# Attention scores of four heads as two full-height products instead of three half-height ones

## The reference, cut to what matters

```
def xattn(x, data):                     # 16 heads of 16 columns
    q = (x @ Wq + bq)                   # [16, 256, 16, 16]
    k, v = split(data @ Wkv + bkv)      # [16, 77, 16, 16] each
    scores = einsum('bqhd,bkhd->bhqk', q, k) / sqrt(16)
    return einsum('bhqk,bkhd->bqhd', softmax(scores), v) @ Wp + bp
x = x + xattn(layernorm(x), ctx)
x = x + moe(layernorm(x))               # 8 experts, top 2, hidden width 1024, gated
```

## Time and profile before

| | |
|---|---|
| runs | 932.6 us median of 3 (931.0 to 934.75) |
| the profiled execution | 938.24 us, of which the span is 936.4 us |
| mean granted TensorE clock | 0.989 |
| busy share of PE, DVE, ACT, POOL | 95%, 80%, 69%, 44% |

### The profile page before, as it was taken

One profiled execution on the slowest core, in us unless ns is written; L12 is line 12 of the kernel. 1 busy time (PEld: TensorE's weight loads), 2 busy tenths in 40 slices (PEclk: granted clock), 3 DMA queues, 4 the chain that ended last, 5 costly groups with the idle time before them and its releaser, 6 DMA issues.

```text
span 936.4 us, 19131 instructions
## 1 busy us (share of the span) xinstructions
PE 887.6 (95%) x6174; PEld 795.6 (85%) x6174; DVE 745.0 (80%) x1757; ACT 646.3 (69%) x1297; POOL 408.9 (44%) x649
## 2 busy tenths in 40 slices
PE   4999999999998998999999999999999999999995
PEld 3888878887877876788999989899898998998994
DVE  2688888888878888787979788887877877778783
ACT  3676766767666774775977777867776776777773
POOL 3456576777776575330432240605114234052052
PEclk8899999999999999999999999999999999999998
DMA  6332333342255337643756455827817838466442
GB/s 144 66 67 49 74 85 69 86 99 61 63 128 177 114 118 268 182 112 121 217 121 185 135 155 168 240 94 186 278 45 215 282 68 259 177 178 177 147 79 27
DMA packets 132368, 129.17 MB, mean 138 GB/s; under 512 B 59936, under 2 KB 117152, under 8 KB 132128
## 3 DMA queue, kind: packets, MB, share of 16 engines
q1 hardware_dynamic: 119392, 110.36, 38.7%
q0 software_dynamic: 12864, 17.44, 10.3%
HBM read 102.01 MB, written 25.36 MB: 136 GB/s over the span
## 4 chain that ended last, share of the span: by engine, by line
PE 78%; DVE 11%; issue 3%; ACT 3%; another core or an unknown queue 1%; POOL 1%; SPq 1%; DMA 0%; POOLq 0%; DVEq 0%; ACTq 0%
PE bank L1985 35%; PE bank L2029 18%; PE bank L1820 5%; PE bank L1737 4%; PE bank L1977 3%; PE bank L1755 3%; PE bank L1774 2%; DVE maxes L1238 2%; PE bank L1784 2%; PE bank L2017 1%; PE bank L1954 1%; DVE probs L1244 1%; DVE q_l L1279 1%; PE bank L1792 1%
## 5 line engine op out<-in xcount | busy, mean ns | idle before, releaser
L852 POOL DMA_INDIRECT out_rows<-yo,token x68 | 114.4, 1682 | 384.9 <-ACT yo L1095 319.8
L1985 PE MATMUL bank<-xh,wh 128*128 128x512 f32 (+1 forms) x672 | 234.7, 349 | 5.4 <-DVE gate_in L1610 4.8
L1985 PE MATMUL bank<-xl,wh 128*128 128x512 f32 (+1 forms) x672 | 228.9, 341 | 0.0
L1985 PE MATMUL bank<-xh,wl 128*128 128x512 f32 (+1 forms) x672 | 228.5, 340 | 0.0
L1586 DVE TENSOR_TENSOR wl<-raw,wh 128x1024 fp32r<-128x1024 f32 x126 | 152.4, 1220 | 13.0 <-ACT wh L1026 12.1
L1985 PEld LDWEIGHTS bank<-xh,wh 128*128 128x128 f32 x672 | 127.9, 190 | 20.1 <-DVE gate_in L1610 7.5
L2029 PE MATMUL bank<-wh,hh 128*128 128x256 f32 x496 | 141.9, 286 | 1.7 <-issue 1.3
L1985 PEld LDWEIGHTS bank<-xh,wl 128*128 128x128 f32 x672 | 127.8, 190 | 14.9
L2029 PE MATMUL bank<-wh,hl 128*128 128x256 f32 x496 | 140.4, 283 | 0.0
L2029 PE MATMUL bank<-wl,hh 128*128 128x256 f32 x496 | 140.4, 283 | 0.0
L1985 PEld LDWEIGHTS bank<-xl,wh 128*128 128x128 f32 x672 | 128.2, 191 | 10.8
(11 more groups left out here) (195 smaller groups left out, 1861.6 us busy)
## 6 DMA issues: line engine op xcount, KB each, us to landing
raw<-in_W SPq DMA_DIRECT2D x42, 1024.0 KB
raw<-in_Wo SPq DMA_DIRECT2D x25, 1024.0 KB
whole<-in_W SPq DMA_DIRECT2D x8, 1024.0 KB, 7.6
xs<-in_x SPq DMA_DIRECT2D x32, 128.0 KB, 2.7
out_rows<-x SPq DMA_DIRECT2D x32, 128.0 KB, 1.8
shared<-z_rows SPq DMA_DIRECT2D x7, 520.0 KB
bo_row<-in_bo SPq DMA_DIRECT2D x25, 128.0 KB
k_blocks<-k_parts SPq DMA_DIRECT2D x128, 19.2 KB
```

Source lines behind the costliest of these rows:

```text
L852: e.indirect_dma_start(out=out, out_offset=bass.IndirectOffsetOnAxis(ap=token[j % 4][:, s:s + 1], axis=0), in_=yo[j % 2][:, s, :], in_offs ...
L1985: mm = e.matmul(ps[:, h * cols:(h + 1) * cols], ws[split_before(j) % 2][:, w, c, m * P:(m + 1) * P], xx[j % 2][:, c, 0:cols], start=(h == ...
```

## The change: what it does

- The queries of a batch are kept as `q_parts[P, m, g, SEQ]`: for group `g`, the high part stands on the group's own 64 partitions and the low part on the other 64. ACT writes the high parts in two instructions of 64 partitions instead of one of 128, DVE the low parts likewise, onto the other half of the partitions.
- The keys get two tiles a batch: `k_hi` has the high blocks on both halves of the partitions, `k_lo` the low blocks on the group's own half, zeros on the other. One matmul of 128 rows with `k_hi` gives high by high plus low by high; one with `k_lo` gives high by low. `k_lo` lies in the third part of the expert weight tiles `wh[0]` and `wl[0]`, which is unused in this stage.
- `scores(i, m)` issues four matmuls of 128 rows, two for group 0, then two for group 1. Each group waits for its own bank.
- `spread_keys(b)` issues 24 DMAs instead of 8, each of 16 partitions with 2 runs of 77 numbers. POOL clears four tiles of 1232 columns instead of two.

```diff
+KEY_PIECES = 3 * HPC
...
+        k_hi = [sb(f"k_hi{i}", [P, DC, 2, HPB, CTX], F32R) for i in range(2)]
+        k_lo = [part[0][:, 2, :, :].rearrange("p c n -> p (c n)")[
+            :, 0:DC * 2 * HPB * CTX].rearrange("p (m g h k) -> p m g h k", m=DC, g=2, h=HPB)
+                for part in (wh, wl)]
+        q_parts = [sb(f"q_parts{i}", [P, DC, 2, SEQ], F32R) for i in range(2)]
...
                 for h in range(HPC):
+                    g, j = divmod(h, HPB)
                     part = slice(h * HD, (h + 1) * HD)
-                    e.dma_start(k_blocks[b % 2][part, :, :, h % HPB, :].bitcast(F32),
-                                k_parts[part, :, :, b % 2, :].bitcast(F32)).then_inc(
-                                    f_kblocks[b % 2], 16)
+                    other = slice((1 - g) * HALF + j * HD, (1 - g) * HALF + (j + 1) * HD)
+                    for rows_of, dst, w in ((part, k_hi, 0), (other, k_hi, 0), (part, k_lo, 1)):
+                        e.dma_start(dst[b % 2][rows_of, :, g, j, :].bitcast(F32),
+                                    k_parts[part, w, :, b % 2, :].bitcast(F32)).then_inc(
+                                        f_kblocks[b % 2], 16)
...
-                e.activation(q_h[b % 2][:, :, :], q_t[:, :, :], ACTF.Copy).then_inc(q_high, 1)
+                for g in range(2):
+                    part = slice(g * HALF, (g + 1) * HALF)
+                    e.activation(q_parts[b % 2][part, :, g, :], q_t[part, :, :],
+                                 ACTF.Copy).then_inc(q_high, 1)
...
-                e.wait_ge(q_high, b + 1)
-                e.tensor_tensor(q_l[b % 2][:, :, :], q_t[:, :, :],
-                                q_h[b % 2][:, :, :].bitcast(F32), ALU.subtract).then_inc(q_low, 1)
+                for g in range(2):
+                    part = slice(g * HALF, (g + 1) * HALF)
+                    other = slice((1 - g) * HALF, (2 - g) * HALF)
+                    e.wait_ge(q_high, 2 * b + g + 1)
+                    e.tensor_tensor(q_parts[b % 2][other, :, g, :], q_t[part, :, :],
+                                    q_parts[b % 2][part, :, g, :].bitcast(F32),
+                                    ALU.subtract).then_inc(q_low, 1)
...
-                if u0 >= 2:
-                    e.wait_ge(less_max, u0 - 1)
-                for k, (qs, w) in enumerate(((q_h, 0), (q_l, 0), (q_h, 1))):
-                    for g in range(2):
-                        mm = e.matmul(
-                            score_bank[(u0 + g) % 3][:, 0:HPB * CTX],
-                            qs[b % 2][g * HALF:(g + 1) * HALF, m, s * P:(s + 1) * P],
-                            k_blocks[b % 2][g * HALF:(g + 1) * HALF, w, m, :, :].rearrange(
-                                "p h k -> p (h k)"), start=(k == 0), stop=(k == 2))
-                        if k == 2:
-                            mm.then_inc(scores_mm, 1)
+                for g in range(2):
+                    if u0 + g >= 3:
+                        e.wait_ge(less_max, u0 + g - 2)
+                    for k, ks in enumerate((k_hi, k_lo)):
+                        mm = e.matmul(score_bank[(u0 + g) % 3][:, 0:HPB * CTX],
+                                      q_parts[b % 2][:, m, g, s * P:(s + 1) * P],
+                                      ks[b % 2][:, m, g, :, :].rearrange("p h k -> p (h k)"),
+                                      start=(k == 0), stop=(k == 1))
+                    mm.then_inc(scores_mm, 1)
```

More of the change, by code:

```diff
@@ L373, in build @@
         v_rep = [sb(f"v_rep{i}", [P, KB, VW]) for i in range(2)]
-        k_blocks = [sb(f"k_blocks{i}", [P, 2, DC, HPB, CTX], F32R) for i in range(2)]
-        q_h = [sb(f"q_h{i}", [P, DC, SEQ], F32R) for i in range(2)]
-        q_l = [sb(f"q_l{i}", [P, DC, SEQ], F32R) for i in range(2)]
+        k_hi = [sb(f"k_hi{i}", [P, DC, 2, HPB, CTX], F32R) for i in range(2)]
[3 more added lines that the diff above has]
+        q_parts = [sb(f"q_parts{i}", [P, DC, 2, SEQ], F32R) for i in range(2)]
         v_blocks = [sb(f"v_blocks{i}", [P, KB, BLOCK_HEADS, VW]) for i in range(2)]
@@ L510, in spread_keys @@
                 e.wait_ge(k_low, b // 2 + 1)
-                if b == 0:
-                    e.wait_ge(blocks_ready, 2)
+                if b < 2:
+                    e.wait_ge(blocks_ready, 2 * b + 2)
                 if b >= 2:
@@ L806, in pool_program @@
             for i in range(2):
-                e.memset(k_blocks[i][:, :, :, :, :].bitcast(F32), 0.0).then_inc(blocks_ready, 1)
+                for blocks in (k_hi, k_lo):
+                    e.memset(blocks[i][:, :, :, :, :].bitcast(F32), 0.0).then_inc(blocks_ready, 1)
             e.memset(half[:, :], -0.5).then_inc(half_ready, 1)
@@ L899, in keys @@
                     for fl in f_kblocks:
-                        e.wait_ge(fl, 16 * HPC * t)
+                        e.wait_ge(fl, 16 * KEY_PIECES * t)
                 else:
@@ L922, in queries @@
                 if b:
-                    e.wait_ge(q_low, b)
+                    e.wait_ge(q_low, 2 * b)
                 else:
@@ L1729, in scores @@
                 if s == 0 and m == 0:
-                    e.wait_ge(q_low, b + 1)
-                    e.wait_ge(f_kblocks[b % 2], 16 * HPC * (b // 2 + 1))
+                    e.wait_ge(q_low, 2 * b + 2)
+                    e.wait_ge(f_kblocks[b % 2], 16 * KEY_PIECES * (b // 2 + 1))
                 u0 = 4 * i + 2 * m
-                if u0 >= 2:
-                    e.wait_ge(less_max, u0 - 1)
-                for k, (qs, w) in enumerate(((q_h, 0), (q_l, 0), (q_h, 1))):
-                    for g in range(2):
-                        mm = e.matmul(
-                            score_bank[(u0 + g) % 3][:, 0:HPB * CTX],
-                            qs[b % 2][g * HALF:(g + 1) * HALF, m, s * P:(s + 1) * P],
-                            k_blocks[b % 2][g * HALF:(g + 1) * HALF, w, m, :, :].rearrange(
-                                "p h k -> p (h k)"), start=(k == 0), stop=(k == 2))
-                        if k == 2:
-                            mm.then_inc(scores_mm, 1)
+                for g in range(2):
[7 more added lines that the diff above has]
+                    mm.then_inc(scores_mm, 1)
             def transpose_probs(i, g):
```

## The result

The changed kernel takes 1074.9 us (median of 5; 1072.4 to 1076.5) against 932.6: a ratio of 1.151, interval 1.148 to 1.155. The forecast was 991 us, at most 1020: right in sign and in the part that loses (SP's pieces), wrong in size and in the wait through which they act.

The account below looks back on a forecast made before the run. PE, 95% busy, was taken to bound the kernel. The profiled 938.2 us plus 44 for 13 periods, 9 start, 1 batches 1 and 2, 4 end made 996; the median, 5.6 lower, 991 us. Range 962 to 1020.

Parts of the forecast that it names:

- SP decides: SP's queue: 24 key-piece issues a batch instead of 8, 14.9 us, expected to decide the outcome.
- Pitch 0.57 us, between 0.51 and 0.64: SP's key pieces: time from one issue to the next, giving 13.7 us for 24, 14.9 us with disturbance.
- rivals (1) and (2): SP's queue: issues hidden, 925 us, chance 0.08; or issue time scaling with runs, 952 us, chance 0.10.
- Now the loop.: Attention batches: pieces, values, POOL, shift, `y`, next pieces span two periods; period 21.1 us instead of 17.7, +44 us.
- waits costed at nothing: New waits on POOL, DVE and ACT for things done long before; ACT's for 24 pieces up to 1 us.
- POOL waits for the values 5 us or more in every batch, `y` waits for the shift: Expected signs: POOL's `v_blocks` waits 5 us or more each batch, ACT's `y` waits for the shift every even round.
- 3 us idle in each batch, clock perhaps: PE in each batch: idle some 3 us in a row, with the clock possibly falling.
- rival (3): PE: as forecast, and the clock falls too, 1.7 us of work lost a batch, +22 us, 1013 us; chance 0.12.
- PE's slot 0.2 us shorter, 13 us; waits, 5 us: PE's 64 score slots: four full-height matmuls save 13 us, separate bank waits 5 us, if PE stays the bound.
- DVE +16 us: DVE's split low-query instruction: about 1.0 us a batch on the path, 16 us, between 0 and 20.
- Start +9 us, batches 1 and 2 +1: Stage start: longer first pieces and clearing, +9 us (6 to 12); batches 1 and 2 +1 (0 to 3).
- End +4: After the last pieces: layer norm later, less slack and what is regained, +4 us (2 to 6).

Follow-up runs that it names:

- e1: The changed kernel with only the high key pieces on the group's own partitions, 8 key DMAs a batch instead of 24; 932.7 us, ratio 0.991 to the kernel before.
- e5: The kernel before with 16 more small DMAs a batch, each behind a key piece and copying into an unused place; 1085.1 us, one run.
- e3: The changed kernel with the 24 key pieces issued behind the loads of the values instead of ahead of them; 1147.0 us, one run.
- e4: The changed kernel with 120 small matmuls before each batch's first scores, from batch 1 on, keeping PE busy; 1077.0 us, one run.
- e8: e1 with whole 128-partition query instructions on ACT and DVE and one wait ahead of both groups; ratio 0.994 to the kernel before.
- e6: e1 with ACT's high and DVE's low queries in one 128-partition instruction each, separate waits kept; ratio 0.993 to the kernel before.
- e7: e1 with one wait for both banks ahead of both groups, query instructions still split; ratio 1.001 to the kernel before.
- v3: The changed kernel with 8 key DMAs a batch, high blocks copied by two SP DMAs, odd batches' pieces early; 961.0 us, ratio 1.029 to the kernel before.

## Why the prediction was wrong, by its steps

- *SP decides.* Right: e1 and e5 show that the issues carry the whole loss.
- *Pitch 0.57 us, between 0.51 and 0.64.* It is the upper end, 0.637: the number of runs makes no difference between two and four, and what sets it apart from the 0.47 us behind `wp` is not shown. 15.5 us for a batch instead of 14.9; rivals (1) and (2), which let small pieces be cheap, fell with it.
- *"Now the loop."* This step failed. I followed the pieces to the values behind them, POOL, the shift and `y`, a loop over two periods, and got 21.1 us. I left out the shortest way: the pieces themselves, the scores that read them, x1 of that round, the next pieces. That loop closes in one period. From the trace of before it could be had, at full clock: 15.5 + 1.3 + 8.3 = 25.1 us; 26.4 was measured, and the other 1.3 us are those of the half clock behind the wait. Among the waits costed at nothing I had named ACT's wait for the pieces and not PE's. The 5.3 us missed in each of 13 periods are 69 us of the 80 by which the profiled execution passed the sum of 996: some 4.0 of the 5.3 are the path and 1.3 the clock. Of the rest 10 us lie ahead of batch 2 and 1 behind batch 15.
- *POOL waits for the values 5 us or more in every batch, `y` waits for the shift.* The first came (13 waits, 125.9 us), the second in 6 cases for 6.2 us in all. By the prediction's own signs ("if `y` doesn't wait") this spoke against it. A wait can be there and cost nothing; e3 took it away and the last scores came 69 us later.
- *3 us idle in each batch, clock perhaps.* This was rival (3). PE is idle for 7.9 us, and the clock falls in every batch. It cost 1.3 us a period by the table (9.59 against 8.28 before and 8.19 in e4), 17 us in all, near the 1.7 that the rival put on it; it lies on top of the path. The stretches agree with what the page "TensorE: Matmul & The Clock Gate" of the Trainium skill, section "Loop structure matters more than you think", says of a long wait.
- *PE's slot 0.2 us shorter, 13 us; waits, 5 us.* The products alone gave 0.6% (e8), some 6 us, with the separate waits 0.7% (e6) to 0.9% (e1). The slot itself was mis-sized: in e8 from the first product to the next work it is 0.65 us, about the 0.62 of before, though the 0.18 us gap behind it is gone. Where e8's gain comes from I haven't settled; the first group's result is there after two products instead of after five.

```profile
151.99 0.39 PE L1748 MATMUL bank<-k_hi,q_parts 128*128 128x308 f32 x1
...
152.64 0.38 PE L1801 MATMUL bank<-const,xn 128*128 128x128 f32 x2
```

- *DVE +16 us.* On the path 0 with separate waits, some 7 us with one (e7 against e8); an instruction of 64 x 512 took 0.69 us on average, not 0.96.
- *Start +9 us, batches 1 and 2 +1.* The first scores came 10.4 us later, and the time from batch 1's pieces to batch 2's grew by 9.2 us more: the same loop already holds there. *End +4:* it was 5 us.

## What to carry to other kernels

When DMAs are added to a queue, follow each of them to its first reader and compare with the time at which it is ready, before following what stands behind them in the queue: here 9.9 us of issue met 2.4 us of slack. A queue that is idle half of the time has no slack if its idle time lies before the release and the reader stands right behind it. Count issues, not bytes: a change that saves TensorE 6 us can't pay for 16 issues a batch at 0.64 us. Whether it pays with the added pieces issued from another engine's queue, no run here tries.

## What the runs showed of the hardware

- A DMA inside the core of 16 partitions holds SP for 0.593 us with 2 runs of 308 bytes each and for 0.596 with 4 (medians). The page "DMA: Bandwidth & Descriptors" of the Trainium skill, section "Issuing engines are not separate DMA queues", says that the time to initiate a DMA is usually small relative to the DMA itself. Here the 24 issues of a batch take 12 times the 1.3 us of landing behind the last of them, and are what counts.
- Behind a copy inside the core of 64 partitions x 2 runs of 1232 bytes PE could start 2.3 to 3.8 us after the end of its issue, behind a key piece 1.3 us after (v3; the change).
- After 7.9 us of idle PE, the next 6 us of work were granted 0.50; with 120 small matmuls in each wait the clock was 0.97 on average over the batches.
